# Edge passes of a graph network: one block in four of the equality matrices converted on Pool instead of ScalarE

## The chip, the cores and the metric

The kernel runs on one core of a Trainium2 chip. The metric is the device time of one execution in microseconds (us), the median of several runs. Engines are called TensorE (PE in the profile; PEld is its weight load), VectorE (DVE), ScalarE (ACT), Pool (POOL, also GpSimd) and SyncE (SP), which here only issues transfers. ACTq and SPq are the transfer-issuing sides of ScalarE and SyncE.

## The reference

A stack of four graph layers over 3125 nodes with 128 features and 50,000 edges, sorted by destination. Ahead of each layer stands `h = relu(layernorm(x))`, behind it `x = x + layer(h)`.

```
layer 0   gcn:   agg = segment_sum((h*norm_out) @ W [src], dst);  layernorm, relu, + h
layer 1   attn:  8 heads of 16; logits = sum(q[dst] * (k[src] + e)) / 4;  softmax over the edges of a dst
                 agg = segment_sum(alpha * (v[src] + e), dst);  + skip, layernorm, feed-forward, layernorm
layer 2   gat1:  3 heads of 128; e = leaky_relu(el[src] + er[dst]);  softmax over the edges of a dst
                 out = segment_sum(alpha * feat[src], dst) + residual;  elu
          gat2:  the same with 1 head of 128
layer 3   sage:  two layers: segment mean of h[src] over dst, two linear maps, scale and shift
```

The three softmax-weighted sums over edges (attn, gat1, gat2) are the kernel's edge passes. Each needs, for every edge, a row of a table gathered at `src`, a logit, the maximum of the logits over the edges of its destination, an exponential, and a sum over the edges of its destination.

## The kernel before, in words

The edges lie in 392 blocks of 128, one edge per partition; four blocks are a group (GC = 4), so there are NG = 98 groups. For each block an equality matrix says which of its 128 edges share a destination. These matrices are made once, in bf16, and kept in device memory (same_hbm, 128 KB per group). In every edge pass each group's four matrices are loaded again, converted to f32 and used as the weights of TensorE: the product with the messages gives, at each edge, the sum over all edges of its block with the same destination.

An edge pass (`edge_pass(p)`, one on each engine) runs over the 98 groups like this:

- SP: `load_group(g)` loads the matrices into same_b, a ring of four slots (UNROLL = 4), in attn also the edge features and the destination rows. A slot is loaded anew once its conversion four groups back is done. Ahead of the first group SP fetches what starts the pass: in attn the rows of q at the first edge of a run of edges, in gat1 and gat2 the whole table starts_er.
- Pool: gathers the table rows of the group by `src`, one indirect DMA per block, so four per group (L1032), into row_b, a ring of eight (RB = 8). Ahead of them it gathers first_rows (L1019). Group n waits in attn for `dst_done` of group n-2 (AHEAD = 2), in gat1 and gat2 for `sum_done` of group n-7 (BEHIND = 7), and from group 8 on also for the messages of group n-8.
- ScalarE: `same_f32(g)` converts same_b to same_f, a ring of eight (one instruction of 128x512; the helper `copy`, L1063, is the line of all ScalarE copies), `exps(i)` takes the exponentials, `evac(g)` copies the sums from PSUM, `store_ends(g)` sends them to device memory.
- TensorE: in attn `attr_t`, `edge_terms` (L1584) and `dst_rows` (L1594; it reads same_f); in all passes `logit_t` (L1602), `max_t` (L1609) and `sums(g)` (L1620; it reads same_f as weights and the messages).
- VectorE: `terms(g)` (L2230 to L2247 in attn, L2238 and L2251 in gat1 and gat2) needs the gathered rows; `maxima(i)` (two scans), `difs(i)` and `messages(g)` (L2290).

The order on each engine comes from `ticks`: a tick i covers the groups 2i and 2i+1, and each stage stands at an offset from it.

```
VectorE          maxima(i-1), terms(2i), difs(i-1), terms(2i+1), messages(2i-2), messages(2i-1)
ScalarE gat      evac(2i-4), keep_max(i-1), exps(i-1), evac(2i-3), same_f32(2i+3), same_f32(2i+4), stores
TensorE gat      logit_t(i-1), sums(2i-4), max_t(i-1), sums(2i-3)
```

Between engines stand semaphores; `Count.at(p, g, back)` is the value that one has once group g - back is done, and `RingSignal` the same for the rings of loads, where a semaphore counts 16 per transfer.

Of the kernel before, what the change touches and what calls it, by code (L numbers as in the profile page):

```python
# [21 lines left out]
GC = 4  # L22
NG = -(-E // (P * GC))
# [10 lines left out]
UNROLL = 4  # L34
# [23 lines left out]
RB = 8  # L58
# [120 lines left out]
def gnn_stack_kernel(nc, out, x, src, dst, edge_attr_64, **w):  # L179
    ctx = ExitStack()  # L180
    with ctx:
# [3 lines left out]
        def sem(name):  # L185
            return ctx.enter_context(nc.semaphore(name))
# [120 lines left out]
        same_f = place(11748, P, RB, GC, P)  # L307
# [85 lines left out]
        same_b = sb("same_b", [P, UNROLL, GC, P], BF16)  # L393
# [72 lines left out]
        exp_done = Count(sem("exp_done"), wp, NPR)  # L466
        msg_done = Count(sem("msg_done"), wp, NG)
        same_f_done = Count(sem("same_f_done"), wp, NG)
        sum_done = Count(sem("sum_done"), wp, NG)
        evac_done = Count(sem("evac_done"), wp, NG)  # L470
        dst_done = Count(sem("dst_done"), ("attn",), NG)
# [160 lines left out]
        def _(sp):  # L632
# [151 lines left out]
            def edge_pass(p):  # L784
                c = chains["x_" + p]
                W = width(p)
                heads = WEIGHTED[p][0]
                v_attr = eattr.rearrange("(g k p) c -> g p k c", k=GC, p=P)
                v_st = starts["attn"][0:EP, :].rearrange("(g k p) c -> g p k c", k=GC, p=P)

                cs = chains["s_" + p]
                sp.wait_ge(s_gather, scatters[p])
                if p == "attn":
                    sp.wait_ge(s_firsts, firsts[p])
                    sp.wait_ge(s_steps, cs.at("firsts"))
                    load(starts[p][0:EP, :].rearrange("(a t e) c -> t a e c", a=QA, e=P)[:, :, P - 1, :],
                         first_rows[:, :, 0:starts[p].shape[1]])
                else:
                    sp.wait_ge(s_store, stores[p])
                    sp.wait_ge(s_steps, cs.at("er_in"))  # L800
                    load(goes_on[:, :, :], breaks[0:CH, 0:P].rearrange("(a t) e -> t a e", a=QA))
                    load(er_r[:, :, 0:P * starts[p].shape[1]],
                         starts[p][0:EP, :].rearrange("(a t e) c -> t a (e c)", a=QA, e=P))
                landed()
                sp.sem_inc(s_steps, 1)

                def load_breaks(i):
                    if i >= UNROLL:
                        sp.wait_ge(max_done.sem, max_done.at(p, i, UNROLL))
                    v = breaks[i * PB:(i + 1) * PB, 0:P + 1].rearrange("k (a e) -> k a e", a=1)  # L810
                    sp.dma_start(brk_b[0:PB * heads, i % UNROLL, :],
                                 v.to_broadcast([PB, heads, P + 1])).then_inc(brk_in.of(i), 16)

                def load_group(g):
                    r = g % UNROLL
                    if g >= UNROLL:
                        sp.wait_ge(same_f_done.sem, same_f_done.at(p, g, UNROLL))
                    sp.dma_start(same_b[:, r, :, :], same_hbm[g].rearrange("p (k c) -> p k c", k=GC))\
                      .then_inc(same_in.of(g), 16)
                    if p == "attn":  # L820
                        if g >= UNROLL:
                            sp.wait_ge(attr_t_done.sem, attr_t_done.at(p, g, UNROLL))
                        sp.dma_start(at_b[:, r, :, :], v_attr[g]).then_inc(attr_in.of(g), 16)
                        if g >= UNROLL:
                            sp.wait_ge(dst_done.sem, dst_done.at(p, g, UNROLL))
                        sp.dma_start(q_b[:, r, :, :], v_st[g]).then_inc(starts_in.of(g), 16)

                for g in range(NG):
                    if g % 2 == 0:
                        load_breaks(g // 2)  # L830
                    load_group(g)
                for g in (NG - 2, NG - 1):
                    sp.wait_ge(ends_out.of(g), ends_out.at(p, g))
                sp.wait_ge(s_steps, c.at("z_in"))
                v = ends[p][0:EP, :].rearrange("(a t e) c -> t a e c", a=QA, e=P)
                load(z_rows[:, :, 0:W], v[:, :, 0, :])
                load(f_rows[:, :, 0:W], v[:, :, P - 1, :])
                landed()
                sp.sem_inc(s_steps, 1)
                sp.wait_ge(col_out, col_at(p, col_chunks(p)))  # L840
                load(ends[p][EP + P:EP + P + CH, :].rearrange("(a t) c -> t a c", a=QA), r_rows[:, :, 0:W])
                landed()
                sp.sem_inc(s_steps, 1)
# [39 lines left out]
        def _(pool):  # L883
            c = chains["prep"]
            g = nc.gpsimd
# [128 lines left out]
            def edge_pass(p):  # L1014
                dst_tab = q_tab if p == "attn" else er_tab[p]
                c2 = dst_tab.shape[1]
                pool.wait_ge(s_store, stores[p])
                for a in range(QA):
                    g.indirect_dma_start(out=first_rows[:, a, 0:c2], out_offset=None, in_=dst_tab,  # L1019
                                         in_offset=bass.IndirectOffsetOnAxis(ap=first_i[:, a:a + 1], axis=0))\  # L1020
                     .then_inc(s_firsts, 16)
                for n in range(NG):
                    if p == "attn" and n >= AHEAD:
                        pool.wait_ge(dst_done.sem, dst_done.at(p, n, AHEAD))
                    elif p != "attn" and n >= BEHIND:
                        pool.wait_ge(sum_done.sem, sum_done.at(p, n, BEHIND))
                    if n >= RB:
                        pool.wait_ge(rows_in.of(n), rows_in.at(p, n, 1))
                        pool.wait_ge(msg_done.sem, msg_done.at(p, n, RB))
                    for k in range(GC):  # L1030
                        at = n * GC + k
                        g.indirect_dma_start(out=row_b[:, n % RB, k, 0:row_tab[p].shape[1]], out_offset=None,  # L1032
                                             in_=row_tab[p],
                                             in_offset=bass.IndirectOffsetOnAxis(ap=src_i[:, at:at + 1], axis=0))\
                         .then_inc(rows_in.of(n), 16)

                pool.wait_ge(s_steps, chains["x_" + p].end)
                av = agg_of(p)
                for j in range(NJ):
                    for t in range(*TURNS[j]):  # L1040
                        g.indirect_dma_start(out=av[:, t, :], out_offset=None, in_=ends[p],
                                             in_offset=bass.IndirectOffsetOnAxis(ap=end_i[:, t:t + 1], axis=0))\
                         .then_inc(agg_in[j], 16)
# [15 lines left out]
        def _(act):  # L1059
            a = nc.scalar  # L1060

            def copy(o, i):
                return a.activation(o, i, ACT.Copy)  # L1063
# [107 lines left out]
            def edge_pass(p):  # L1171
# [33 lines left out]
                def same_f32(g):  # L1205
                    act.wait_ge(same_in.of(g), same_in.at(p, g))
                    if g >= RB:
                        act.wait_ge(sum_done.sem, sum_done.at(p, g, RB))
                    copy(same_f[:, g % RB, :, :], same_b[:, g % UNROLL, :, :]).then_inc(same_f_done.sem, 1)

                def evac(g):
                    act.wait_ge(sum_done.sem, sum_done.at(p, g))
# [167 lines left out]
        def _(pe):  # L1380
# [174 lines left out]
            def edge_pass(p):  # L1555
# [31 lines left out]

                def dst_rows(g):
                    pe.wait_ge(same_f_done.sem, same_f_done.at(p, g))
                    if g >= 2:  # L1590
                        pe.wait_ge(prod_done.sem, prod_done.at(p, g, 2))
                    pe.wait_ge(starts_in.of(g), starts_in.at(p, g))
                    for k in range(GC):
                        i = mm(bank((3, 7)[g % 2])[:, k * D:(k + 1) * D], same_f[:, g % RB, k, :],  # L1594
                               q_b[:, g % UNROLL, k, :], start=True, stop=True)
                    i.then_inc(dst_done.sem, 1)
# [15 lines left out]
                def sums(g):  # L1612
                    pe.wait_ge(msg_done.sem, msg_done.at(p, g))
                    if p != "attn":
                        pe.wait_ge(same_f_done.sem, same_f_done.at(p, g))
                    if g >= 1:
                        pe.wait_ge(evac_done.sem, evac_done.at(p, g, 1))
                    for k in range(GC):
                        o = bank(4 + k)[:, 0:W] if p == "gat1" else bank(4 + k // 2)[:, (k % 2) * 256:(k % 2) * 256 + W]
                        i = mm(o, same_f[:, g % RB, k, :], msg[:, g % 4, k * W:(k + 1) * W], start=True, stop=True)  # L1620
                    i.then_inc(sum_done.sem, 1)
# [970 lines left out]
```

## Time and profile before

| | us |
|---|---|
| median of three timed runs | 3223.82 |
| lowest and highest | 3223.29, 3227.91 |
| profiled execution, its own time | 3249.72 |
| span of the profile (first to last instruction) | 3248.1 |
| TensorE, VectorE, Pool, ScalarE busy | 2206.5, 1424.8, 1352.2, 955.5 |
| gathers of attn, gat1 and gat2, first to last (from the span's start) | 665.9 to 1261, 1436 to 2013, 2216 to 2777 |

The profiled execution is 26 us longer than the median of the timed runs; durations and places all come from the profiled one. Busy time is that of instructions that compute, and for Pool that of its indirect transfers too; the time of issuing other transfers and of waiting is not in it. The idle time in brackets behind an instruction is that of its engine just before it, with what ended it; "issue" is time for which the profile shows no wait, and "remote" one whose releaser the profile doesn't name.

### The profile page before, as it was taken

Reading aid. Unit: us, or ns where it says so; the run is one execution under the profiler, and the core shown is the slowest. Engines: PE = TensorE matmul, PEld = TensorE weight load, DVE = VectorE, ACT = ScalarE, POOL = GpSimd, SP = SyncE. Lnnn points to the kernel's source line nnn. Section 1 sums busy time; section 2 is a strip of 40 time slices with the busy share of each in tenths; the row PEclk is TensorE's granted clock in tenths of the full one; section 3 lists DMA queues with packets and bytes.
Section 4 is the critical chain, followed back from the end, with each engine's and each line's share of the span. In section 5 each row is a group of like instructions: output and inputs, shape, how many; then the busy total and the mean of one; then the engine's idle time right before and its main releaser. Section 6 shows DMA issues by size and latency. Waiting matters only on the chain.

```text
span 3248.1 us, 33280 instructions
## 1 busy us (share of the span) xinstructions
PE 2206.5 (68%) x10859; PEld 1539.8 (47%) x10859; DVE 1424.8 (44%) x3094; ACT 955.5 (29%) x2050; POOL 1352.2 (42%) x1417
## 2 busy tenths in 40 slices
PE   4899999657888787545566666673334343379998
PEld 3566666346767675332233333352333333346666
DVE  5765553636556555633444334322222222341413
ACT  2522221422333232543333333231222222120202
POOL 3000000566666663476666665226666666210000
PEclk9777778878778886768888888785555555589999
DMA  9378852168777774125666666313545454356361
GB/s 219 110 264 271 287 200 85 66 176 231 219 226 225 222 224 133 26 64 168 201 205 208 205 193 198 108 30 78 119 106 125 107 123 111 117 159 196 114 203 55
DMA packets 518582, 517.96 MB, mean 159 GB/s; under 512 B 153344, under 2 KB 463763, under 8 KB 517227
## 3 DMA queue, kind: packets, MB, share of 16 engines
q1 hardware_dynamic: 310349, 267.63, 27.2%
q0 software_dynamic: 50528, 115.22, 14.1%
q10 hardware_dynamic: 157534, 132.98, 13.0%
q8 instruction: 89, 1.46, 0.2%
q14 instruction: 82, 0.67, 0.1%
HBM read 301.53 MB, written 227.32 MB: 163 GB/s over the span
## 4 chain that ended last, share of the span: by engine, by line
PE 43%; issue 15%; another core or an unknown queue 14%; DVE 9%; ACT 8%; POOL 5%; DMA 4%; ACTq 1%; SPq 0%; DVEq 0%; POOLq 0%
PE ps L1620 9%; PE ps L1551 9%; PE ps L1445 7%; PE ps L1455 6%; ACT arena L1063 5%; POOL arena L1032 3%; DMA ends_gat<-arena 3%; PE ps L1584 2%; PE ps L1594 2%; PE ps L1533 2%; DVE arena L1940 1%; PE ps L1576 1%; PE ps L1800 1%; PE ps L1648 1%
## 5 line engine op out<-in xcount | busy, mean ns | idle before, releaser
L1620 PE MATMUL ps<-arena 128*128 128x136 f32 (+2 forms) x2352 | 697.4, 460 | 649.8 <-ACT arena L1063 386.5
L1063 ACT ACTIVATE arena<-ps 128x544 f32<-128x544 f32 (+9 forms) x591 | 484.7, 825 | 1577.6 <-remote 598.4
L1032 POOL DMA_INDIRECT arena<-t_gat,src_i x784 | 742.0, 946 | 396.0 <-issue 222.7
L1620 PEld LDWEIGHTS ps<-arena 128*128 128x128 f32 x2352 | 477.9, 268 | 820.4 <-issue 727.5
L1032 POOL DMA_INDIRECT arena<-t_attn,src_i x392 | 376.2, 960 | 219.4 <-issue 105.0
L1551 PE MATMUL ps<-arena 128*128 128x384 bf16 x1850 | 305.7, 329 | 39.0 <-DVE rec L2446 36.5
L2274 DVE TENSOR_TENSOR dif<-logit,ps 128x64 f32<-128x64 f32 (+2 forms) x147 | 27.6, 187 | 590.4 <-remote 321.9
L2290 DVE TENSOR_TENSOR arena<-arena,ps 128x1536 f32<-128x1536 f32 (+1 forms) x196 | 230.5, 1218 | 95.4 <-issue 57.4
L1551 PEld LDWEIGHTS ps<-arena 128*128 128x128 bf16 x1850 | 182.1, 99 | 162.4 <-issue 45.2
L991 POOL TENSOR_TENSOR arena<-arena,r_L_gnn_gamma 128x512 f32<-128x512 f32 (+1 forms) x7 | 8.1, 1153 | 539.2 <-ACT arena L1263 539.1
L1455 PE MATMUL ps<-arena 128*128 128x100 bf16 x1176 | 224.5, 364 | 9.4 <-DVE arena L2070 9.2
L1445 PE MATMUL ps<-arena 128*128 128x385 bf16 x925 | 219.8, 411 | 0.0
L1455 PEld LDWEIGHTS ps<-arena 128*128 128x128 bf16 x1176 | 169.4, 145 | 59.0 <-DVE arena L2070 12.5
L2261 DVE TENSOR_TENSOR_SCAN arena<-arena,ps 64x128 f32<-64x128 f32 (+2 forms) x147 | 59.9, 408 | 281.1 <-remote 203.3
L1063 ACT ACTIVATE arena<-same_b 128x512 f32<-128x512 bf16 x294 | 167.5, 620 | 28.0 <-DMA same_b<-same_hbm 27.4
L1445 PEld LDWEIGHTS ps<-arena 128*128 128x128 bf16 x925 | 111.7, 121 | 102.3 <-issue 67.7
L1063 ACT ACTIVATE arena<-arena 128x512 bf16<-128x512 f32 (+4 forms) x208 | 63.9, 307 | 277.8 <-DVE arena L2542 246.5
L1584 PE MATMUL ps<-w_e,arena 64*128 64x128 f32 x784 | 134.9, 321 | 0.0
L2542 DVE TENSOR_REDUCE arena<-ps 128x128 f32<-128x384 f32 x74 | 36.2, 550 | 220.1 <-PE ps L1551 220.1
L2230 DVE TENSOR_TENSOR arena<-arena,ps 128x1024 f32<-128x1024 f32 x98 | 118.0, 1204 | 29.1 <-PE ps L1594 28.1
L1594 PE MATMUL ps<-arena 128*128 128x128 f32 x784 | 130.0, 316 | 0.0
L1584 PEld LDWEIGHTS ps<-w_e,arena 64*128 64x128 f32 x784 | 114.3, 221 | 25.6 <-issue 25.5
(321 smaller groups left out, 2671.5 us busy)
## 6 DMA issues: line engine op xcount, KB each, us to landing
ends_gat<-arena ACTq DMA_DIRECT2D x98, 774.0 KB
arena<-adj_hbm SPq DMA_DIRECT2D x90, 640.0 KB, 4.0
same_b<-same_hbm SPq DMA_DIRECT2D x294, 128.0 KB
adj_hbm<-arena SPq DMA_DIRECT2D x9, 3200.0 KB, 11.8
ends_attn<-arena ACTq DMA_DIRECT2D x98, 272.0 KB
ends_gat<-arena ACTq DMA_DIRECT2D x98, 258.0 KB
arena<-edst SPq DMA_DIRECT2D x98, 256.0 KB, 4.4
starts_q<-zrow SPq DMA_DIRECT2D x28, 896.0 KB, 6.8
```

The source lines that it names most:

```text
L1032: g.indirect_dma_start(out=row_b[:, n % RB, k, 0:row_tab[p].shape[1]], out_offset=None, in_=row_tab[p], in_offset=bass.IndirectOffsetOnAxi ...
L1063: return a.activation(o, i, ACT.Copy)
L1445: i = mm(bank(4 + n % 4)[:, 0:3 * D + 1], lhs, xs0[:, t, 0:3 * D + 1], start=t == 0, stop=t == NT - 1)
L1455: i = mm(ps[:, at:at + KEYS], hot_e[:, b % 3, :, e], hot_k[:, b % 3, :, e], start=True, stop=True)
L1533: i_ = mm(bank(half * 4 + dl)[:, a0 - g0:a1 - g0], l, sel_of[p][:, off + a0:off + a1], start=ch == use[0] and s == 0, stop=ch == use[-1] a ...
L1551: m = mm(bank(ch % 2 * 4 + dl)[:, 0:3 * D], ring[:, u % RING, at:at + P], xs1[:, t, :, :].rearrange("p s c -> p (s c)"), start=t == 0, sto ...
L1584: i = mm(bank((1, 6)[g % 2])[:, k * D:(k + 1) * D], at_t[:, g % 2, k * P:(k + 1) * P], w_e[:, :], start=True, stop=True)
L1594: i = mm(bank((3, 7)[g % 2])[:, k * D:(k + 1) * D], same_f[:, g % RB, k, :], q_b[:, g % UNROLL, k, :], start=True, stop=True)
L1620: i = mm(o, same_f[:, g % RB, k, :], msg[:, g % 4, k * W:(k + 1) * W], start=True, stop=True)
L2230: tt(kv, kv, bc(bank((1, 6)[g % 2]).rearrange("p (k s c) -> p k s c", k=GC, s=1), [P, GC, 2, D]), ALU.add).then_inc(kve_done.sem, 1)
L2261: v.tensor_tensor_scan(fwd[0:kh, s, :], b[:, 0:P], bank(2)[0:kh, 0:P][:, ::-1], -BIG, ALU.add, ALU.max)\
L2290: tt(m[:, :, 0:heads * nc_].rearrange("p k (h c) -> p k h c", h=heads), rows_v, e, ALU.mult).then_inc(msg_done.sem, 1)
```

## The change

The first of the four blocks of a group is converted by Pool, the other three by ScalarE, now in one instruction of 128x384. Pool's copy for group n+1 stands behind the four gathers of group n; the one for group 0 stands ahead of the first gather of the pass. A second semaphore, same_p_done, counts Pool's copies: SP waits for it before it loads a slot of same_b anew, TensorE before dst_rows and, in gat1 and gat2, before sums. Pool's copy waits for the load of the matrices and, from group 8 on, for the sums of eight groups before, which read the same slot of same_f.

```diff
+        same_p_done = Count(sem("same_p_done"), wp, NG)
 ...
                     if g >= UNROLL:
                         sp.wait_ge(same_f_done.sem, same_f_done.at(p, g, UNROLL))
+                        sp.wait_ge(same_p_done.sem, same_p_done.at(p, g, UNROLL))
                     sp.dma_start(same_b[:, r, :, :], same_hbm[g].rearrange("p (k c) -> p k c", k=GC))\
 ...
+                def first_block(m):
+                    pool.wait_ge(same_in.of(m), same_in.at(p, m))
+                    if m >= RB:
+                        pool.wait_ge(sum_done.sem, sum_done.at(p, m, RB))
+                    g.tensor_copy(same_f[:, m % RB, 0, :], same_b[:, m % UNROLL, 0, :]).then_inc(same_p_done.sem, 1)
+
+                first_block(0)
                 for n in range(NG):
 ...
                          .then_inc(rows_in.of(n), 16)
+                    if n + 1 < NG:
+                        first_block(n + 1)
 ...
-                    copy(same_f[:, g % RB, :, :], same_b[:, g % UNROLL, :, :]).then_inc(same_f_done.sem, 1)
+                    copy(same_f[:, g % RB, 1:GC, :], same_b[:, g % UNROLL, 1:GC, :]).then_inc(same_f_done.sem, 1)
 ...
                 def dst_rows(g):
                     pe.wait_ge(same_f_done.sem, same_f_done.at(p, g))
+                    pe.wait_ge(same_p_done.sem, same_p_done.at(p, g))
 ...
                     if p != "attn":
                         pe.wait_ge(same_f_done.sem, same_f_done.at(p, g))
+                        pe.wait_ge(same_p_done.sem, same_p_done.at(p, g))
```

## Rows read from the trace of the kernel before

**Rows 1.** The page, part 1: busy time, share of the span, instructions.
```profile
PE 2206.5 (68%) x10859; PEld 1539.8 (47%) x10859; DVE 1424.8 (44%) x3094; ACT 955.5 (29%) x2050; POOL 1352.2 (42%) x1417
```

**Rows 2.** Busy time by stretch: attn, gat1, gat2, each over its gathers.
```profile
666.00:1265.00 599.00, 474.86 (x2808) 406.86 (x2808) 349.78 (x527) 181.19 (x432) 376.07 (x392) 0.81 0.76 218
1436.00:2018.00 582.00, 340.56 (x848) 172.53 (x849) 235.03 (x445) 207.65 (x380) 371.66 (x392) 0.84 0.62 194
2216.00:2782.00 566.00, 212.85 (x843) 176.97 (x844) 133.61 (x441) 127.36 (x379) 370.45 (x393) 0.50 0.48 113
```

The columns are the stretch, its length, the busy time of PE, PEld, DVE, ACT and POOL with their instructions, the granted clock of TensorE, the transfer share and GB/s.

**Rows 3.** Groups by line, shapes apart: conversions and gathers (busy, mean ns, idle before).
```profile
L1032 POOL DMA_INDIRECT arena<-t_gat,src_i x784 | 742.0, 946 | 396.0 <-issue 222.7 <-remote 125.1 <-PE ps L1620 48.2
...
L1063 ACT ACTIVATE arena<-same_b 128x512 f32<-128x512 bf16 x294 | 167.5, 620 | 28.0 <-DMA same_b<-same_hbm 27.4 <-issue 0.6
```

**Rows 4.** Timeline at the start of gat1 (start, length, instruction, idle before).
```profile
1436.09 0.97 POOL L1032 DMA_INDIRECT arena<-t_gat,src_i  x1 [0.30 <-issue]
...
1439.85 0.44 SPq L818 DMA_DIRECT2D same_b<-same_hbm  x1
...
1457.86 0.17 DVE L2238 TENSOR_TENSOR z_b<-arena 128x12 f32<-128x12 f32 x1 [1.93 <-DMA arena<-t_gat,src_i]
```

**Rows 5.** Timeline at the start of gat2.
```profile
2216.43 0.97 POOL L1032 DMA_INDIRECT arena<-t_gat,src_i  x1 [0.30 <-issue]
...
2219.75 0.82 SPq L818 DMA_DIRECT2D same_b<-same_hbm  x2
...
2237.83 0.18 DVE L2238 TENSOR_TENSOR z_b<-arena 128x4 f32<-128x4 f32 x1 [4.52 <-DMA arena<-t_gat,src_i]
```

**Rows 6.** Timeline at the start of attn.
```profile
665.85 0.97 POOL L1032 DMA_INDIRECT arena<-t_attn,src_i  x1 [0.30 <-issue]
...
670.40 0.45 SPq L818 DMA_DIRECT2D same_b<-same_hbm  x1
...
673.12 0.63 ACT L1063 ACTIVATE arena<-same_b 128x512 f32<-128x512 bf16 x1 [26.77 <-DMA same_b<-same_hbm]
...
682.26 1.22 DVE L2230 TENSOR_TENSOR arena<-arena,ps 128x1024 f32<-128x1024 f32 x1 [28.07 <-PE ps L1594]
682.44 0.94 POOL L1032 DMA_INDIRECT arena<-t_attn,src_i  x1 [6.87 <-PE ps L1594]
```

**Rows 7.** Timeline in the middle of gat2, two places.
```profile
2493.98 0.60 ACT L1063 ACTIVATE arena<-ps 128x516 f32<-128x516 f32 x1 [3.83 <-remote]
...
2494.72 2.06 PE L1620 MATMUL ps<-arena 128*128 128x129 f32 x8 [3.20 <-issue]
...
2504.59 0.60 ACT L1063 ACTIVATE arena<-ps 128x516 f32<-128x516 f32 x1 [7.91 <-remote]
...
2504.83 0.94 POOL L1032 DMA_INDIRECT arena<-t_gat,src_i  x1 [3.25 <-remote]
...
2554.55 0.94 POOL L1032 DMA_INDIRECT arena<-t_gat,src_i  x1 [0.30 <-issue]
...
2557.80 0.13 DVE L2238 TENSOR_TENSOR z_b<-arena 128x4 f32<-128x4 f32 x1
```

**Rows 8.** Groups by line, shapes apart: ScalarE's widest evacuation.
```profile
L1063 ACT ACTIVATE arena<-ps 128x1548 f32<-128x1548 f32 x98 | 143.2, 1461 | 375.4 <-PE ps L1620 177.0 <-remote 121.7 <-issue 55.4
```

**Rows 9.** Groups by line, shapes apart: Pool's instructions of 128x128.
```profile
L1005 POOL TENSOR_TENSOR h_sb<-h_sb,r_L_gnn_bskip 128x128 f32<-128x128 f32 x1 | 0.9, 907 | 0.0
...
L905 POOL TENSOR_SCALAR_AFFINE_SELECT ident<-ident 128x128 f32<-128x128 f32 x1 | 0.3, 292 | 0.2 <-POOL grp_row L902 0.2
...
L886 POOL MEMSET x_sb<- 128x128 f32 x1 | 0.2, 205 | 0.3 <-POOLq L2583 0.3
```

**Rows 10.** Timeline of Pool ahead of gat1: between transfers and tensor_tensors (no bracket: no idle).
```profile
1411.63 0.96 POOL L983 DMA_INDIRECT starts_er<-er_all,start_i  x1 [0.31 <-issue]
1412.60 1.28 POOL L991 TENSOR_TENSOR arena<-arena,r_L_gnn_g 128x512 f32<-128x512 f32 x1
...
1415.38 1.45 POOL L983 DMA_INDIRECT starts_er<-er_all,start_i  x1 [0.15 <-issue]
```

**Rows 11.** The tile same_b: time from issue to landing of its loads.
```profile
DMA to landing us min/median/max: 1.7/3.6/12.9
```

## The prediction

> **What bounds the kernel now.** The change touches only the three edge passes (attn, gat1, gat2), so I read the busy times first, then the passes by stage, then the start and the middle of a pass instruction by instruction. Over the whole run no engine is full: TensorE 68%, VectorE 44%, ScalarE 29%, Pool 42% [rows 1]. The stretches of the passes [rows 2] show the same: in gat1 ScalarE is busy 207.65 of 582 us and Pool 371.66; in gat2 127.36 and 370.45 of 566. So these are loops of latencies, and what counts is which wait ends last.
>
> The two engines that the change trades between stand like this. ScalarE converts a group's matrices 294 times at 620 ns; its idle time before these is 28.0 us, of which 27.4 us is a wait for the data [rows 3], nearly all in one place at the start of attn. Pool issues 784 + 392 gathers; the gat gathers take 946 ns each [rows 3] and follow each other with 0.30 us between, so 1.25 us apart and 5.0 us for a group of four. A group takes 582/98 = 5.9 us in gat1 and 566/98 = 5.8 us in gat2 [rows 2]: Pool runs at 85% of its own pace.
>
> At the start of gat1 Pool begins to gather at 1436.09, 3.76 us before SP even issues the first load of same_b at 1439.85 [rows 4]; SP had first to fetch the starts table. VectorE takes group 3 at 1457.86 and had sat idle 1.93 us for its rows. Gat2 is the same: first gather at 2216.43, first same_b load at 2219.75, and group 3 taken at 2237.83 after 4.52 us of waiting for rows [rows 5]. In both passes the first messages wait for group 3 (tick 1 does the maxima, terms 2, differences, terms 3, then messages 0 and 1), so here the gather stream sets the end. In attn it doesn't: Pool stops after two groups and idles 6.87 us until 682.44, when TensorE has done the first destination rows [rows 6].
>
> In the middle of a pass Pool waits for TensorE: after a run of 16 gathers it idles 3.25 us until 2504.83; ScalarE, which evacuates the same sums, was idle 7.91 us until 2504.59 [rows 7]. The sums began at 2494.72 and by their modelled length end 2.06 us later, so the release comes 7.8 us later than the profile's matmul end; the profile doesn't show why.
>
> **The change part by part.** (a) ScalarE's conversion goes from 512 to 384 columns. From 1461 ns for 1548 columns [rows 8] and 620 ns for 512 [rows 3] a column costs 0.81 ns, so 128 columns are 0.10 us, and 294 of them 31 us. On the path I count nothing of it: the conversions run while ScalarE waits for the next sums (idle 3.83 us before the evacuation at 2493.98, 7.91 us before the next [rows 7]). If that cover were gone it would be worth all 31 us.
>
> (b) Pool gets 294 copies of 128x128, bf16 to f32. The trace has no such copy. From below, a 128x128 memset takes 205 ns; from above, a two-input 128x128 tensor_tensor takes 907 ns; nearest is the one-input affine_select at 292 ns [rows 9]. Between two gathers Pool idles 0.30 us anyway; from a gather into a tensor_tensor there is no gap, and from a tensor_tensor into a gather 0.15 us [rows 10]. So a copy between two gathers adds 0.29 + 0.15 - 0.30 = 0.14 us; bounds 0.06 and 0.76 us. A group then takes Pool 5.14 us, still under 5.8.
>
> In the middle of a pass this has cover. The copy for group n+1 stands behind the gathers of n and ahead of the wait for sums, so the copy of the group that is held up falls into the idle 3.25 us. The group with the least to spare is that one: its gathers end at 2555.49 and it is taken at 2557.80, 2.31 us later [rows 7], where a group whose rows were being waited for came 1.6 us after its last gather (group 3 of gat2: 16 gathers from 2216.43 at 1.25 us end at 2236.2, taken at 2237.83 [rows 5]). The copies of the other three groups of a run add 0.42 us to 20 us and come out of the 3.25 us of idle. Counted: 0. At the bound of 0.76 us they add 2.3 us, also less than the idle.
>
> (c) New waits. Pool's copy of group m waits for same_in(m) and for sum_done(m-8). The second is no new wait: gat's gathers m-1 have waited for sum_done(m-8) already, and in attn TensorE does those sums ahead of the dst_done(m-3) that gathers m-1 wait for. SP's reload of a slot also waits for Pool's copy four groups back, some 23 us before Pool needs the slot's next contents; a load lands in a median of 3.6 and at most 12.9 us [rows 11], so no stall in the middle. TensorE's sums and destination rows wait for Pool's copy as well; in gat it stands ahead of the same group's gathers, so long before; in attn it follows gathers g-1, which start on dst_done(g-3), while three groups take 3 x 6.1 us and Pool needs 5.2. Counted: 0.
>
> (d) The one that costs: first_block(0) stands ahead of the first gather, and behind it on Pool's queue is the whole gather stream. Now Pool can't start until same_b(0) has landed. In attn ScalarE, idle and waiting for just that load, started 673.12 - 670.40 = 2.72 us after SP's issue [rows 6]. With this, gat1's first gather goes from 1436.09 to 1439.85 + 2.72 + 0.29 + 0.15 = 1443.01, which is 6.92 us later; three more copies before group 3's last gather make it 7.34. As VectorE was waiting for these rows [rows 4] the whole amount goes through to the first messages. Gat2: 2219.75 + 3.16 = 2222.91 against 2216.43, 6.48, with the copies 6.90 [rows 5]. Nothing later takes it back, since the loop behind it is bound by its own latencies and not by how far Pool is ahead. Attn: the first gather goes from 665.85 to 670.40 + 3.16 = 673.56, 7.7 us later; group 0 is through at 678.6 and its rows by 680.2, ahead of 682.2 when VectorE can take it; Pool ends group 1 at 683.7, so group 2 starts at 683.7 instead of 682.44, and Pool's next waits absorb that. Counted: 0.
>
> **The sum.** 7.3 + 6.9 = 14.2 us. The profiled execution took 3249.72 us around a span of 3248.1; it would take 3263.9. The three timed runs have a median of 3223.82, 26 us less than the profiled one; I take the same 14.2 us there: 3238.0.
>
> The Trainium skill (SBUF — State Buffer, the part on the two sides and the shared port pair) says that VectorE, in an instruction with two SBUF inputs, and a GpSimd instruction that reads SBUF exclude each other for their whole length. No row here shows such a pair collide. By that rule a few copies and VectorE instructions are put off; its price from rows is the fourth rival below, and the sum above goes without it.
>
> **The rivals.** *Pool sets the period* (0.16). In gat2 the release comes again and again some 3 us after Pool runs dry, as in rows 7, whatever TensorE started in between. If the release hangs on Pool's run, and not only Pool on the release, every run of 16 gathers gets longer by its three inner copies: 0.42 us x 24.5 runs x 3 passes = 31 us, so 3269; with copies at 0.76 us it would be 168 us more. Against it: Pool has 15% idle, and VectorE waits for rows only at the starts.
>
> *No loss at the start* (0.09). If the later start only uses up Pool's lead, and the first sums are held back anyway as they are later in the pass (7.8 us beyond their length, rows 7), the 14 us vanish: 3224. Against it: group 3 itself was waited for, and it is what the first messages need.
>
> *ScalarE's time is on the path* (0.12; the other side). If the conversions hold up the evacuations, 31 us come back and outweigh the start: 3223.8 + 14.2 - 31 = 3207. It decides from about half of the conversions on the path. Against it: the idle time behind them in rows 7.
>
> *Collisions of the port* (0.08): VectorE's instructions with two SBUF inputs in gat last some 0.5 us of a 5.8 us group (z_b, logit and a scan of 0.41), so a 0.29 us copy meets one in (0.5 + 0.29)/5.8 = 14% of 196 groups, for at most 0.4 us: 11 us more, 3249. This is what the Trainium skill's rule on that page would do.
>
> **How the numbers follow.** The forecast, 3238, has 0.55. A measurement of this kernel tells some 0.2% (6.4 us) from no change: below 3217.4 is faster, above 3230.3 slower. Faster 0.12, same 0.09, slower 0.55 + 0.16 + 0.08 = 0.79. The range leaves out the ScalarE case (0.12) and the part of the Pool case with a dear copy (about 0.06): from 3220, under the case of no loss, to 3278. The likeliest case alone: 3231 to 3246, from a load that lands in 1.7 to 5 us.
>
> **What would show it.** Right: gat1's and gat2's first gathers stand right behind the first copy and about 7 us after the last first_rows gather; group 3's terms come some 7 us later, counted from that point; a copy takes near 0.3 us; Pool's idle before the held-up group shrinks from 3.3 to some 2.9 us while the run-to-run period stays at 23 us; ScalarE's conversions at about 0.52 us with more idle behind them. Wrong: a period that grows with the copies, copies well above 0.5 us, VectorE waiting for rows in the middle of a pass, or passes of the old length from the first gather's old place.

## The result, and the profile after

| | us |
|---|---|
| before, median of 13 runs | 3224.48 (3215.1 to 3232.9) |
| after, median of 13 runs | 3243.1 (3229.8 to 3256.6) |
| ratio after to before, 95% interval | 1.0055 (1.0039 to 1.0071) |
| forecast | 3238.0 (3220 to 3278) |

The change costs 0.55%, some 18 us (12.6 to 22.9 by the interval); 14.2 were forecast. Single executions lie up to 9 us from their median before and up to 14 us after. The two profiled ones show it: the changed kernel's has a span of 3243.0 us, 5 us less than the span of before, though it is the slower kernel. So below, lengths within a stretch are compared, and totals only by ratios of many runs. Times that two traces give for one place differ by where their spans stand; I count from the last first_rows gather of a pass, which no part of the change moves.

Busy times from the page of the changed kernel, which answer to [rows 1]:

```profile
PE 2213.5 (68%) x10859; PEld 1550.3 (48%) x10859; DVE 1430.2 (44%) x3094; ACT 922.9 (28%) x2050; POOL 1445.5 (45%) x1711
```

Pool has 294 instructions and 93 us more, ScalarE 33 us less. The groups by line and shape, which answer to [rows 3]:

```profile
L1041 POOL DMA_INDIRECT arena<-t_gat,src_i x784 | 744.5, 950 | 327.8 <-issue 197.2 <-remote 92.0 <-PE ps L1633 38.6
...
L1028 POOL CAST arena<-same_b 128x128 f32<-128x128 bf16 x294 | 89.9, 306 | 19.4 <-DMA same_b<-same_hbm 18.7
...
L1074 ACT ACTIVATE arena<-same_b 128x384 f32<-128x384 bf16 x294 | 136.1, 513 | 27.8 <-DMA same_b<-same_hbm 27.8
```

A copy takes 0.31 us, a conversion 0.51 instead of 0.62. Of the copies' idle time 18.7 of 19.4 us is a wait for the load of same_b, and that is three waits: one at the start of each pass. Pool's timeline at the start of gat1, where [rows 4] had no gap before the first gather:

```profile
1426.25 0.96 POOL L1021 DMA_INDIRECT arena<-er_gat,first_i  x1 [0.31 <-issue]
1433.29 0.38 POOL L1028 CAST arena<-same_b 128x128 f32<-128x128 bf16 x1 [6.08 <-DMA same_b<-same_hbm]
1433.82 0.99 POOL L1041 DMA_INDIRECT arena<-t_gat,src_i  x1 [0.16 <-issue]
...
1438.57 0.30 POOL L1028 CAST arena<-same_b 128x128 f32<-128x128 bf16 x1
1439.04 0.97 POOL L1041 DMA_INDIRECT arena<-t_gat,src_i  x1 [0.17 <-issue]
```

SP and VectorE in the same place:

```profile
1431.13 0.91 SPq L820 DMA_DIRECT2D same_b<-same_hbm  x2
```
```profile
1440.23 0.17 DVE L2251 TENSOR_TENSOR z_b<-arena 128x12 f32<-128x12 f32 x1 [5.01 <-DMA arena<-t_gat,src_i]
...
1445.34 0.17 DVE L2251 TENSOR_TENSOR z_b<-arena 128x12 f32<-128x12 f32 x1 [4.73 <-DMA arena<-t_gat,src_i]
...
1450.56 0.17 DVE L2251 TENSOR_TENSOR z_b<-arena 128x12 f32<-128x12 f32 x1 [3.38 <-DMA arena<-t_gat,src_i]
...
1455.73 0.17 DVE L2251 TENSOR_TENSOR z_b<-arena 128x12 f32<-128x12 f32 x1 [4.70 <-DMA arena<-t_gat,src_i]
```

The first gather stands 2.69 us behind SP's load where it stood 3.76 ahead of it. VectorE now waits for the rows of each of the first four groups, one group of Pool apart (5.2 us), where before, of these four in gat1, it waited for group 3's alone. Group 3 is taken 1455.73 - 1426.25 = 29.48 us after the last first_rows gather; before it was 1457.86 - 1434.83 = 23.03. So 6.45 us later. Gat2 is the same, and answers to [rows 5]:

```profile
2207.79 0.96 POOL L1021 DMA_INDIRECT arena<-er_gat,first_i  x1 [0.30 <-issue]
2214.39 0.34 POOL L1028 CAST arena<-same_b 128x128 f32<-128x128 bf16 x1 [5.64 <-DMA same_b<-same_hbm]
2214.89 0.99 POOL L1041 DMA_INDIRECT arena<-t_gat,src_i  x1 [0.16 <-issue]
```
```profile
2236.96 0.17 DVE L2251 TENSOR_TENSOR z_b<-arena 128x4 f32<-128x4 f32 x1 [4.75 <-DMA arena<-t_gat,src_i]
```

That is 29.17 us against 2237.83 - 2215.16 = 22.67: 6.50 later.

In the middle of a pass the loop keeps its period. Two of Pool's waits in gat2 that follow each other stand 2504.83 - 2481.81 = 23.02 us apart before and 2420.72 - 2397.82 = 22.90 after, and the wait itself fell from 3.1 to 3.3 us to some 2.3 (before, whose second wait is in [rows 7], then after; a few others are longer or shorter):

```profile
2481.81 0.94 POOL L1032 DMA_INDIRECT arena<-t_gat,src_i  x1 [3.09 <-remote]
```
```profile
2397.82 0.96 POOL L1041 DMA_INDIRECT arena<-t_gat,src_i  x1 [2.31 <-remote]
...
2420.72 0.96 POOL L1041 DMA_INDIRECT arena<-t_gat,src_i  x1 [2.36 <-remote]
```

VectorE does wait for rows more often in gat2, by the idle time ahead of its first instruction of a group (before, then after):

```profile
L2238 DVE TENSOR_TENSOR z_b<-arena 128x4 f32<-128x4 f32 x98 | 14.7, 150 | 24.3 <-DMA arena<-t_gat,src_i 16.2 <-issue 8.0
```
```profile
L2251 DVE TENSOR_TENSOR z_b<-arena 128x4 f32<-128x4 f32 x98 | 15.0, 154 | 58.5 <-DMA arena<-t_gat,src_i 42.3 <-issue 16.0
```

The second trace of the changed kernel has 33.7 us there, so this differs from one execution to the next. What shrank is Pool's wait for TensorE. The waits of Pool's gathers in the changed kernel (us in total, times, longest):

```profile
POOL arena L1041 <- remote: 128.1, 75, 3.5
POOL arena L1041 <- PE ps L1633: 63.1, 52, 2.5
...
POOL arena L1041 <- PE ps L1606: 23.2, 17, 2.6
```

Together 214 us. The kernel before has 299.6 of these in the trace of the run e8 below, and 287.7 in its first trace:

```profile
POOL arena L1032 <- remote: 201.5, 84, 6.6
POOL arena L1032 <- PE ps L1620: 50.0, 23, 2.4
POOL arena L1032 <- PE ps L1594: 48.1, 27, 7.0
```

The copies came out of this idle time.

### The profile page after: what moved, and what is told of

The parts are those of the page before. It is cut to its first block, busy times and chain, and to the rows that moved or that the text cites. A ratio compares the mean times of both kernels' runs of the same rounds, so it can differ in the third digit from the quotient of the medians.

```text
span 3243.0 us, 34416 instructions
## 1 busy us (share of the span) xinstructions
PE 2213.5 (68%) x10859; PEld 1550.3 (48%) x10859; DVE 1430.2 (44%) x3094; ACT 922.9 (28%) x2050; POOL 1445.5 (45%) x1711
## 4 chain that ended last, share of the span: by engine, by line
PE 47%; issue 15%; POOL 10%; DVE 9%; another core or an unknown queue 8%; ACT 6%; DMA 4%; ACTq 1%; SPq 0%; POOLq 0%; DVEq 0%
PE ps L1633 9%; PE ps L1562 9%; POOL arena L1041 7%; PE ps L1456 7%; PE ps L1466 6%; PE ps L1595 3%; PE ps L1606 3%; ACT arena L1074 3%; DMA ends_gat<-arena 2%; PE ps L1544 2%; PE ps L1587 1%; DVE arena L1953 1%; PE ps L1661 1%; PE ps L1813 1%
## 5 line engine op out<-in xcount | busy, mean ns | idle before, releaser
L1633 PE MATMUL ps<-arena 128*128 128x136 f32 (+2 forms) x2352 | 685.1, 454 | 629.9 <-ACT arena L1074 333.8
L1562 PE MATMUL ps<-arena 128*128 128x384 bf16 x1850 | 306.7, 330 | 42.0 <-DVE rec L2459 39.6
L2287 DVE TENSOR_TENSOR dif<-logit,ps 128x64 f32<-128x64 f32 (+2 forms) x147 | 27.5, 187 | 517.4 <-remote 256.7
L1466 PEld LDWEIGHTS ps<-arena 128*128 128x128 bf16 x1176 | 169.4, 145 | 58.8 <-DVE arena L2083 12.6
L1074 ACT ACTIVATE arena<-same_b 128x384 f32<-128x384 bf16 x294 | 136.1, 513 | 27.8 <-DMA same_b<-same_hbm 27.8
L1595 PE MATMUL ps<-w_e,arena 64*128 64x128 f32 x784 | 141.6, 332 | 1.2 <-issue 1.1
L1606 PE MATMUL ps<-arena 128*128 128x128 f32 x784 | 141.0, 335 | 0.0
L2555 DVE TENSOR_REDUCE arena<-ps 128x128 f32<-128x384 f32 x74 | 36.2, 549 | 221.3 <-PE ps L1562 221.3
L1595 PEld LDWEIGHTS ps<-w_e,arena 64*128 64x128 f32 x784 | 119.4, 230 | 26.9 <-issue 26.6
```

The costliest lines, as they stand in the source:

```text
L1466: i = mm(ps[:, at:at + KEYS], hot_e[:, b % 3, :, e], hot_k[:, b % 3, :, e], start=True, stop=True)
L1562: m = mm(bank(ch % 2 * 4 + dl)[:, 0:3 * D], ring[:, u % RING, at:at + P], xs1[:, t, :, :].rearrange("p s c -> p (s c)"), start=t == 0, sto ...
L1595: i = mm(bank((1, 6)[g % 2])[:, k * D:(k + 1) * D], at_t[:, g % 2, k * P:(k + 1) * P], w_e[:, :], start=True, stop=True)
```

## The experiments

Theory: the whole loss is the later start of the gathers, and copies and conversions are hidden. Rivals: the copies slow the loop of a pass (Pool's period, or collisions with VectorE), and ScalarE's saving is worth something that hides a part of a larger loss. All kernels were timed in five rounds against the kernel before, three batches on three chips, on which the kernel before had medians of 3223.44, 3251.41 and 3246.65. Only the ratios can be set beside each other.

The table has for each kernel its ratio, and the time from the last first_rows gather to the first sums of each pass in its trace (before: 25.12 in gat1, from 1434.83 to 1459.95).

| kernel | ratio, 95% interval | attn | gat1 | gat2 |
|---|---|---|---|---|
| before, and again as e8 | 1.0010 (0.9997 to 1.0022) | 36.2, 36.4 | 25.1, 25.3 | 23.7, 23.8 |
| after, and again as e10 | 1.0055 (1.0039 to 1.0071), 1.0055 (1.0036 to 1.0074) | 39.3, 39.5 | 31.6, 31.9 | 30.2, 29.4 |
| e1 copies late | 1.0019 (0.9995 to 1.0042) | 36.0 | 25.9 | 24.8 |
| e2 wait alone | 1.0031 (1.0013 to 1.0049) | 39.0 | 31.2 | 28.7 |
| e3 ScalarE's part alone | 1.0017 (0.9994 to 1.0040) | 36.6 | 24.7 | 23.6 |
| e4 early load | 1.0026 (1.0009 to 1.0044) | 39.2 | 26.9 | 24.6 |
| e5 three copies, late | 0.9996 (0.9983 to 1.0010) | 36.3 | 27.7 | 26.5 |
| e6 start later still | 1.0072 (1.0054 to 1.0090) | 39.6 | 34.8 | 32.2 |
| e7 copy and two memsets, late | 1.0019 (1.0009 to 1.0029) | 39.5 | 27.1 | 25.6 |
| e9 five copies, late | 1.0240 (1.0220 to 1.0260) | 34.4 | 30.1 | 28.9 |
| e11 one first_rows gather | 0.9990 (0.9977 to 1.0003) | 39.6 | 30.9 | 23.9 |

In gat1 and gat2 e11 has one first_rows gather only, and its times count from that; from the first of its four the kernel before has 28.9 and 27.5. From the first to the last sums the three passes take 1700 to 1726 us together in every trace but e9's, in no order of the kernels, so a single trace can't say whether a later start goes through to the end of the pass whole. That rests on the ratios.

**e1, the copies without the late start.**

```diff
-                first_block(0)
 ...
-                    if n + 1 < NG:
+                    late = 1 if p == "attn" else 2
+                    if n == late:
+                        for m in range(late + 1):
+                            first_block(m)
+                    if n >= late and n + 1 < NG:
                         first_block(n + 1)
```

> The whole change, but Pool's first copies of a pass stand behind the gathers of group 1 (attn) or group 2 (gat1, gat2) instead of ahead of the first gather, so that Pool waits for no load of same_b before it gathers. Late-start theory (the later first gather is all the cost): the 14 to 19 us come back, 3224 to 3228 us, ratio to before 1.000 to 1.001, with the first gathers again ahead of SyncE's first same_b load. Pool sets the period (31 us for inner copies): the ratio stays at 1.005 to 1.01. Port collisions (11 us): 1.003. ScalarE on the path: if the shorter conversions gave something back all along, it now shows alone, 0.991 to 0.997.

The first sums are back to within 1.1 us of before in all three passes, and the ratio is 1.0019, no longer to be told from no change. Of 18 us some 12 are gone, by the middle of the interval; the inner copies are all still there.

**e2, the wait without the copies**, in the kernel before:

```diff
+                pool.wait_ge(same_in.of(0), same_in.at(p, 0))
                 for n in range(NG):
```

> The kernel before with one line more: Pool waits for same_b of group 0 ahead of the first gather of each pass. No copy on Pool, ScalarE converts all four blocks. Late-start theory: 14 us more (6.9 in gat1, 6.5 in gat2, 0 in attn), ratio 1.004; VectorE waits for rows in the first groups of gat1 and gat2. No loss at the start (the later gathers only use up a lead): ratio 1.000. Pool sets the period, port collisions: both need the copies, so 1.000 as far as they are the cause of the measured +19 us.

One wait, 3 times in the whole run, costs 1.0031, 10 us (4 to 16). The trace shows first sums 2.8, 6.0 and 5.0 us later in attn, gat1 and gat2, 13.8 us in sum. By these numbers the wait is more than half of the 18 us; whether it is all of it, the intervals don't say. The gat1 start:

```profile
1415.85 0.96 POOL L1019 DMA_INDIRECT arena<-er_gat,first_i  x1 [0.30 <-issue]
1423.43 1.15 POOL L1033 DMA_INDIRECT arena<-t_gat,src_i  x1 [6.61 <-DMA same_b<-same_hbm]
```

**e3, ScalarE's part alone**: 128x384 conversions in the kernel before, and nobody converts block 0.

```diff
-                    copy(same_f[:, g % RB, :, :], same_b[:, g % UNROLL, :, :]).then_inc(same_f_done.sem, 1)
+                    copy(same_f[:, g % RB, 1:GC, :], same_b[:, g % UNROLL, 1:GC, :]).then_inc(same_f_done.sem, 1)
```

> The kernel before with ScalarE converting only blocks 1 to 3 of a group and nobody block 0 (that block's matrix holds stale values; the instructions, their shapes and their waits are otherwise those of before). It prices what the change takes off ScalarE by itself: 294 conversions at 0.51 instead of 0.62 us. My theory: ratio 1.000, the 31 us go into ScalarE's idle time. ScalarE on the path: 0.990 to 0.997.

The conversions take 136.0 us instead of 167.5, and the ratio is 1.0017 (0.9994 to 1.0040): what the change takes off ScalarE is worth nothing, at most 2 us of the 31.

**e4, the whole change with the load of same_b early** in gat1 and gat2:

```diff
                 cs = chains["s_" + p]
+                for r in range(UNROLL if p != "attn" else 0):
+                    sp.dma_start(same_b[:, r, :, :], same_hbm[r].rearrange("p (k c) -> p k c", k=GC))\
+                      .then_inc(same_in.of(r), 16)
                 sp.wait_ge(s_gather, scatters[p])
```

> The whole change, but SyncE issues the same_b loads of groups 0 to 3 of gat1 and gat2 as the first thing of the pass, ahead of its waits for the scatters and of the loads of starts; Pool's first copy then finds its block landed. Late-start theory: the first gathers stand where they stood before plus 0.3 us for a copy, and the 14 to 19 us come back, ratio 1.000 to 1.001. Pool sets the period: 1.005 to 1.01. Port collisions: 1.003.

Pool's wait in gat1 is gone, the copy stands right behind the last first_rows gather:

```profile
1425.03 0.96 POOL L1025 DMA_INDIRECT arena<-er_gat,first_i  x1 [0.31 <-issue]
1425.99 0.30 POOL L1032 CAST arena<-same_b 128x128 f32<-128x128 bf16 x1
1426.46 0.99 POOL L1045 DMA_INDIRECT arena<-t_gat,src_i  x1 [0.17 <-issue]
```

The first sums of gat1 and gat2 come 1.8 and 0.9 us later than before instead of 6.5 each, those of attn still 3.1, where the load isn't moved. In gat1 the rest isn't Pool's: VectorE takes group 0 19.1 us after the last first_rows gather, before it was 16.2, and finds the rows of all four groups there. In sum 5.7 us, and the ratio says 8 (3 to 14). More than half of the loss is back with every copy in its place.

**e5 and e7, more work on Pool** in the form of e1, in a spare tile that nobody reads:

```diff
+        spare = sb("spare", [P, RB, 2, P], BF16)
 ...
+                    for x in range(2):
+                        g.tensor_copy(spare[:, m % RB, x, :], same_b[:, m % UNROLL, 0, :])
                     g.tensor_copy(same_f[:, m % RB, 0, :], same_b[:, m % UNROLL, 0, :]).then_inc(same_p_done.sem, 1)
```

and for e7 `g.memset(spare[:, m % RB, x, :], 0.0)` in the loop.

> As e1 (first copies of a pass behind the gathers of group 1 or 2), but Pool makes three copies a group instead of one: two more of 128x128 bf16 into a spare tile that nobody reads, some 0.3 us each, so about 0.6 us more a group, 58 us more of Pool's time a pass and 176 us in all. If Pool's idle time absorbs copies (my theory), e1's +5 us hardly grows: ratio to before 1.001 to 1.005, as Pool's idle before the held-up group shrinks from some 3 to 1 us. Pool sets the period (each run of 16 gathers grows by its copies): 88 to 176 us more, 1.03 to 1.055. Port collisions: three times the 11 us, 1.010.

> As e5, but the two additional instructions are memsets of the spare tile, 128x128 bf16, which read no SBUF. If what Pool's copies cost is Pool's own time, this costs what e5 costs in proportion to the length of the instructions (a memset takes some 0.2 us by the rows). If it is collisions of an SBUF read with VectorE's two-input instructions, this costs no more than e1, ratio 1.002, while e5 stands near 1.010.

Three copies a group, 242 us on Pool in all, and the time is that of before. Pool's waits in e5:

```profile
POOL arena L1043 <- remote: 47.0, 53, 1.6
POOL arena L1043 <- PE ps L1639: 33.9, 45, 1.7
...
POOL arena L1043 <- PE ps L1612: 4.5, 3, 2.0
```

Of 300 us of such waits some 85 are left, and that is where the copies went. VectorE waits for rows in about half of the groups of gat2, and even that costs nothing that the ratio shows:

```profile
L2257 DVE TENSOR_TENSOR z_b<-arena 128x4 f32<-128x4 f32 x98 | 16.4, 167 | 184.1 <-DMA arena<-t_gat,src_i 177.9 <-issue 3.3 <-ACT arena L1080 2.9
```

The form has its own late start: nine copies of groups 0 to 2 stand ahead of group 3's gathers, and the first sums come 2.6 us later in gat1 and 2.8 in gat2. One for one that would be 5 us, and the ratio allows 3 at most. So a later first sum doesn't always cost its full length. e7's memsets (222 ns each) read nothing and can't be what a read collides with; they come out a little dearer than e5's copies (1.0019 against 0.9996), not cheaper, so nothing here speaks for collisions as the cost. e7's attn start is 3 us late without a reason that I found, and so is that of e11 below.

**e9, five copies**, which by arithmetic are more than Pool's idle time holds. Shown against e5; Pool also waits for its own last copy of the group before, which is long done by then:

```diff
-        spare = sb("spare", [P, RB, 2, P], BF16)
+        spare = sb("spare", [P, 2, 4, P])
 ...
+                    if m >= 1:
+                        pool.wait_ge(same_p_done.sem, same_p_done.at(p, m, 1))
+                    for x in range(4):
+                        g.tensor_copy(spare[:, m % 2, x, :], same_b[:, m % UNROLL, 0, :])
```

> As e5, with five copies a group on Pool instead of three (four of them of 128x128 bf16 to f32 into a spare tile). By the rows of the runs so far a group of Pool then takes 4 x 1.26 + 5 x 0.30 + 0.16 = 6.7 us, against a group period of 5.9 us in attn and gat1 and 5.7 in gat2. If Pool's idle time is the only cover of the copies, it is used up and Pool sets the period: (6.7 - 5.9) x 98 x 2 + (6.7 - 5.7) x 98 = 255 us more, ratio to before 1.06 to 1.08. If copies cost nothing for another reason than Pool's idle time (they overlap the transfers' processing, say), the ratio stays near 1.000.

The direction was right and the size wrong. Pool's gathers by line, and one group of Pool in gat1:

```profile
L1045 POOL DMA_INDIRECT arena<-t_gat,src_i x784 | 745.9, 951 | 211.7 <-issue 181.3 <-POOL arena L1033 29.5 <-PE ps L1641 0.6
```
```profile
1706.79 0.97 POOL L1045 DMA_INDIRECT arena<-t_gat,src_i  x1 [0.16 <-POOL arena L1033]
...
1710.56 0.95 POOL L1045 DMA_INDIRECT arena<-t_gat,src_i  x1 [0.30 <-issue]
1711.51 1.00 POOL L1032 CAST spare<-same_b 128x128 f32<-128x128 bf16 x4
1712.45 0.28 POOL L1033 CAST arena<-same_b 128x128 f32<-128x128 bf16 x1
1712.90 0.97 POOL L1045 DMA_INDIRECT arena<-t_gat,src_i  x1 [0.16 <-POOL arena L1033]
```

Copies behind each other overlap: four take 1.00 us, so a group of Pool is 1712.90 - 1706.79 = 6.11 us and not 6.7. Pool has no idle left, and 98 groups of 6.11 us are 599 us, which is the length of gat1's and gat2's gathers in this trace (599.2 and 598.6; e8: 582.1 and 562.5). With attn (623.3 against 598.7) that is 24.5 + 17.1 + 36.1 = 78 us, and 1.0240 is 78 us. (Against the first trace of the kernel before, with 594.4, 575.5 and 560.0, it would be 91, so the match is no closer than that.) So Pool does set the period once its group is longer than that of the loop, and not before: the rival of the period is a matter of size, and with one copy the size is not reached.

**e6, the start later still**: the whole change, with four copies of 128x512 into a spare tile ahead of the first copy of gat1 and gat2.

```diff
+                if p != "attn":
+                    pool.wait_ge(same_in.of(0), same_in.at(p, 0))
+                    for x in range(4):
+                        g.tensor_copy(spare[:, x, :], same_b[:, 0, :, :].rearrange("p k c -> p (k c)"))
                 first_block(0)
```

> The whole change, and ahead of the first copy of gat1 and of gat2 Pool copies group 0's four blocks four times into a spare tile (4 x 128x512), about 1 us each by the 128x512 row, so the first gathers of both passes start some 4 to 5 us later still. Late-start theory: each microsecond there is a microsecond of the end, +8 to +10 us over the changed kernel, ratio to before 1.008 to 1.009. No loss at the start: as the changed kernel, 1.0055.

The four copies took 2.70 us and not 4 to 5 (they too are cheaper than the two-input instruction that I had estimated them from):

```profile
1435.53 2.70 POOL L1034 COPY spare<-same_b 128x512 bf16<-128x512 bf16 x4 [6.39 <-DMA same_b<-same_hbm]
1438.18 0.41 POOL L1029 CAST arena<-same_b 128x128 f32<-128x128 bf16 x1
```

Two starts of 2.7 us are 5.4 us, and the ratio goes from 1.0055 to 1.0072, which is 5.5 us. The intervals overlap, so this fits one for one without proving it, and e5 stands against it; the first sums are 2.9 and 2.9 us later than in e10.

**e8 and e10, the two kernels again**, for what a repetition gives:

> The kernel before, unchanged, timed as an experiment: how far apart two measurements of one kernel come. Every theory: 1.000, within 0.2%.

> The changed kernel, unchanged, timed as an experiment on the chip of this batch. Late-start theory and all others: 1.0055 as before, within 0.2%. The sum of the later first sums read from the traces (3.1 + 6.5 + 6.5 = 16 us) would be 1.005.

1.0010 and 1.0055. So +0.1% in this table is nothing, and the loss is the same on another chip.

**e11, a start earlier than before**: three of the four blocks of first rows are left out in gat1 and gat2.

```diff
-                for a in range(QA):
+                for a in range(QA if p == "attn" else 1):
                     g.indirect_dma_start(out=first_rows[:, a, 0:c2], out_offset=None, in_=dst_tab,
```

> The kernel before, with one first_rows gather in gat1 and gat2 instead of four (the other three rows of blocks keep stale values), so that the first row gathers of both passes start 3.8 us earlier. It asks whether the start is on the path to the other side too. If VectorE's waits for the rows of groups 3 to 6 set the first sums, up to 1.9 us come back in gat1 and 3.8 in gat2 (the idle time ahead of group 3's terms in rows 4 and 5), ratio 0.998. If the lead was large enough before: 1.000.

1.0 per mille faster, with no change inside the interval. In gat2 the first sums came 23.9 us after the first (and only) first_rows gather, against 27.5 from the first of the four before: 3.6 of 3.8 us won. In gat1 they came 30.9 against 28.9, later: VectorE took group 0 only 22.9 us after that gather, where it had been 20.0 before. Its rows were not the last to come (its four gathers were through 16.9 us earlier); what is left is the chain of the starts table, which I didn't follow further. Moving the start to the earlier side gains in one pass of two, and too little to be measured.

Attn has in e11 the instructions of before, and yet its first sums come late, 689.33 - 649.70 = 39.6 us where they came 36.2 and 36.4 us after in the two traces of the kernel before:

```profile
649.70 0.96 POOL L1019 DMA_INDIRECT arena<-q_tab,first_i  x1 [0.30 <-issue]
```
```profile
689.33 1.95 PE L1620 MATMUL ps<-arena 128*128 128x136 f32 x7 [0.17 <-issue]
```

No experiment made a version that is faster than the kernel before. With ScalarE's saving worth nothing, e1 and e5, the change without its late first gather, can at best be equal to it.

## Why the forecast held, point by point

- **(a) ScalarE's 31 us, counted 0.** Right, shown by e3. The conversion measured 513 ns, 0.11 us less where 0.10 was estimated.
- **(b) The copy.** 0.31 us where the affine_select gave 0.29, with no gap before it and 0.16 after it, as in [rows 10]. A group of Pool went from 5.00 to 5.2 us (1433.82 to 1439.04 above), where 5.14 was forecast. Counted 0 against 85 us less of Pool's waiting; e5 and e9 show how far the cover reaches: it ends between three and five copies a group, where Pool's own time for a group (6.11 us with five) passes the loop's 5.7 to 6.1.
- **(c) New waits, counted 0.** Right: no wait for same_b's load appears behind the first copy of a pass, and e5, with the same waits, has the time of before.
- **(d) The start.** The step that makes the result, and right in kind; e1, e2, e4 and e6 take it away, take it alone, mend it, and enlarge it. Its sizes: gat1 6.45 where 7.34 was forecast, gat2 6.50 for 6.90. The load landed in 2.2 us, not 2.7, and in gat1 group 3 was taken 1.6 us behind its last gather, where before it was 2.0. Attn was counted 0, and its first sums came 3.1 us later (39.3 against 36.2, much the same in e2, e4, e6 and e10, whose Pool also waits). The step had followed only Pool and the first groups' rows. Counted from SP's first load of same_b, VectorE took group 0 1.5 us later than before (676.06 - 662.72 against 11.86) and group 1 4.7 us later:

```profile
683.03 1.22 DVE L2243 TENSOR_TENSOR arena<-arena,ps 128x1024 f32<-128x1024 f32 x1 [4.31 <-PE ps L1595]
```

  Group 1's rows were hardly what came last, since its gathers ended at 675.3, and in e9, where VectorE waits for attn's rows, it takes them 1.8 to 4.0 us behind the last gather. The profile names TensorE, whose modelled end (676.5) is again long past. All five kernels with the wait have this: group 1 is taken 25.7 to 26.0 us after the last first_rows gather, without the wait 21.2 to 22.4. So the lead in attn isn't free either, by a way that the profile doesn't show. How much of the 3.1 us it makes stays open, though: e7 and e11 have no wait there, take groups 0 and 1 as early as before, and have their first sums at 39.5 and 39.6 all the same. TensorE's granted clock doesn't part the cases either: 20 to 25 us after the last first_rows gather it was 0.50 of full (1.2 GHz) in the changed kernel and e2, and 1.00 (2.4 GHz) in the kernel before, but also in e7 and e11. Gat1 and gat2 measured 13.0 us against 14.2 forecast, with attn 16.1, and the result is 18 (12.6 to 22.9). That the total came out near is in part luck: the two terms of gat were each somewhat too large, and attn, counted 0, may have added the rest.
- **The signs.** Pool's idle time ahead of the held-up group went to 2.3 us and not 2.9, since the held-up group's own copy stands in it too; the distance of 23 us held. "VectorE waiting for rows in the middle of a pass" was named as a sign of being wrong, and it was a poor one: it appears in gat2, and in e5 as 184.1 us without a loss.
- **The rivals.** No loss at the start: out by e2. ScalarE on the path: out by e3. Pool sets the period: out for one copy and for three, true at five. Collisions: they exist (last section), but e5 had three times the copies and no loss that could be measured.

Open is a remainder. The later first sums add up to 13 of the 18 us, or 16 with attn's; the wait alone (e2) cost 10 (4 to 16), and e1 with every inner copy 6 (-2 to 14). What the inner copies cost beside the start is therefore not resolved; e5, with three times as many, allows 3 us at most.

Open is also why TensorE's releases come so much later than its modelled ends, in every one of these kernels ([rows 7] before). Had Pool's run of gathers caused it, a run longer by three copies a group would have lengthened the passes; in e5 it didn't. What e5 changed is how often Pool gets to wait: in gat2 every 52 to 70 us for 1.5 us, instead of every 23 for some 3.2.

## What to carry to other kernels

Look at what stands ahead of the first instruction of a stream, not at the stream. The 294 copies cost nothing that could be measured, since they fit into the idle time of the engine; one wait placed ahead of the first of 392 gathers, three times in the run, cost 10 us (4 to 16) by itself, because the load that it waits for is issued late. A new consumer of an old load should come where that load has landed anyway, one or two groups down the queue, or the load has to move up with it.

Relief for an engine that waits for others may be worth nothing: here it was 31 us of busy time. Added work on an engine is free up to a bound that can be read from the profile: its own time for a group against the period of the loop.

## What the runs showed of the hardware

Pool's copies and VectorE's instructions with two SBUF inputs do get in each other's way. In e9, VectorE and Pool in attn:

```profile
734.97 1.14 DVE L2288 TENSOR_TENSOR_SCAN arena<-arena 64x128 f32<-64x128 f32 x1
...
821.70 1.39 DVE L2311 TENSOR_TENSOR arena<-arena 128x512 f32<-128x512 f32 x2
...
823.46 0.54 DVE L2288 TENSOR_TENSOR_SCAN arena<-arena 64x128 f32<-64x128 f32 x1
```
```profile
734.83 1.00 POOL L1032 CAST spare<-same_b 128x128 f32<-128x128 bf16 x4
...
822.62 1.47 POOL L1032 CAST spare<-same_b 128x128 f32<-128x128 bf16 x4
```

The scan takes 0.41 us when nothing meets it. Started 0.14 us behind a run of four copies it took 1.14, as if it had waited for most of the run. The later run began while VectorE multiplied messages (L2311, two SBUF inputs, until 823.09) and met a scan in its middle; it took 1.47 us instead of 1.00, and that scan 0.54. The scan that reads PSUM beside SBUF (L2282, the same shape) kept its 0.41 throughout. The rule of the Trainium skill (SBUF — State Buffer, the section on the two separate sides) that the one which starts first has the shared port and the other waits, and that two SBUF inputs against a reading GpSimd instruction is such a pair, agrees with this. The rule speaks of one instruction, and here the scan waited through several copies of 0.30 us that stood close behind each other. Its price in the changed kernel is small: the three shapes of this scan take 64.0 us instead of 60.8, the z_b and logit instructions 64.2 instead of 62.4, 5 us of VectorE's time in all (3 in the trace of e10), in which it mostly waits for others.

A copy of 128x512 from bf16 to bf16 takes Pool 0.68 us, about half of its two-input instruction of that size in [rows 10], and copies behind each other are 0.24 us apart for 128x128, less than the 0.30 us of a single one.
